# One of four softmax tiles in every other head has its low half made by GpSimd instead of VectorE

## The reference, cut to what matters

```python
scores = jnp.einsum('bhqd,bhkd->bhqk', q, k) / np.sqrt(Q_HEAD)
attn = jax.nn.softmax(scores, axis=-1)
o = jnp.einsum('bhqk,bhkv->bhqv', attn, v)
out = jnp.einsum('bhsv,Hv->bsH', o, Wo) + bo
```

## Time and profile before

| | |
|---|---|
| median of 3 runs | 1705.82 us (1705.19 to 1707.86) |
| the profiled execution's own time | 1698.23 us |
| its span in the trace | 1696.4 us |
| mean granted clock of TensorE | 0.989 of full speed |
| busy: PE, DVE, ACT, POOL | 95%, 90%, 81%, 56% |

### The profile page before, as it was taken

The page is one execution under the profiler, slowest core; times in us unless marked ns, Lnnn a source line. Parts: engine busy times, 40 slices in busy tenths (PEclk is TensorE's granted clock), DMA queues, the critical chain, the costliest instruction groups (busy, mean ns, idle before and its releaser), DMA issues. The chain is left out here.

```text
span 1696.4 us, 24098 instructions
## 1 busy us (share of the span) xinstructions
PE 1617.4 (95%) x7572; PEld 758.7 (45%) x7572; DVE 1522.8 (90%) x2080; ACT 1371.2 (81%) x1979; POOL 942.5 (56%) x1610
## 2 busy tenths in 40 slices
PE   7979899999999999999999999999999999999899
PEld 6734344444444444444444444444444444444344
DVE  5569898999998999999989999999989999999765
ACT  5668788888887889888979888988879888898422
POOL 3346555666655666666646655665545665564320
PEclk9989999999999999999999999999999999999999
DMA  6469999999999999999989999999999999999611
GB/s 218 155 115 211 203 199 205 206 201 187 201 195 166 201 202 200 200 198 196 202 160 203 196 199 198 199 200 198 196 165 196 204 198 199 194 194 201 145 50 50
DMA packets 1090457, 314.10 MB, mean 185 GB/s; under 512 B 1068352, under 2 KB 1078880, under 8 KB 1090336
## 3 DMA queue, kind: packets, MB, share of 16 engines
q1 hardware_dynamic: 1084288, 296.09, 94.8%
q0 software_dynamic: 6048, 16.52, 4.2%
HBM read 35.71 MB, written 8.39 MB: 26 GB/s over the span
## 5 line engine op out<-in xcount | busy, mean ns | idle before, releaser
L952 ACT ACTIVATE S<-S,shift,unscale 128x1024 f32<-128x1024 f32 x512 | 606.2, 1184 | 145.6 <-DVE shift L1007 144.3
L1000 DVE TENSOR_REDUCE mx<-S 128x1 f32<-128x1024 f32 x512 | 623.2, 1217 | 49.7 <-PE S L851 35.2
L992 DVE TENSOR_TENSOR halves<-S,halves 128x1024 f16<-128x1024 f32 x512 | 623.2, 1217 | 27.7 <-ACT halves L961 15.0
L961 ACT ACTIVATE halves<-S 128x1024 f16<-128x1024 f32 x512 | 526.1, 1027 | 26.0 <-DMA PT<-halves 14.2
L849 PE MATMUL S<-kvTH,qeH 128*128 128x512 f16 x1024 | 396.7, 387 | 19.7 <-DVE halves L992 17.9
L850 PE MATMUL S<-kvTL,qeH 128*128 128x512 f16 x1024 | 391.3, 382 | 0.0
L851 PE MATMUL S<-kvTH,qeL 128*128 128x512 f16 x1024 | 391.0, 382 | 0.0
L787 POOL CAST onormH<-onorm 128x512 fp32r<-128x512 f32 x127 | 77.6, 611 | 488.4 <-DVE onorm L1047 488.4
L862 PE MATMUL O<-PT,kvn 128*128 128x512 f16 x1024 | 241.9, 379 | 0.0
L849 PEld LDWEIGHTS S<-kvTH,qeH 128*128 128x128 f16 x1024 | 99.5, 97 | 255.9 <-DVE halves L992 145.3
L789 POOL TENSOR_TENSOR onormL<-onorm,onormH 64x512 fp32r<-64x512 f32 x127 | 163.6, 1288 | 10.2
(11 more groups left out here) (263 smaller groups left out, 1989.4 us busy)
## 6 DMA issues: line engine op xcount, KB each, us to landing
weff_whole<-weff_scratch POOLq DMA_DIRECT2D x126, 128.0 KB, 4.6
PT<-halves SPq DMA_TRANSPOSE x512, 4.9
raw<-in_raw SPq DMA_DIRECT2D x8, 772.0 KB, 5.9
weff_scratch<-w_split SPq DMA_DIRECT2D x8, 512.0 KB, 6.3
x<-in_x SPq DMA_DIRECT2D x4, 1024.0 KB, 8.3
x_all<-in_x SPq DMA_DIRECT2D x3, 1024.0 KB, 6.4
out<-y SPq DMA_DIRECT2D x3, 1024.0 KB, 4.3
wv<-in_wv SPq DMA_DIRECT2D x4, 512.0 KB, 5.1
```

The costliest lines, as they stand in the source:

```text
L952: nc.scalar.activation(S[:, t % SLOTS, :], S[:, t % SLOTS, :], ACT.Exp, bias=shift[:, col:col + 1], scale=keep["unscale"][:, 0:1], accum_o ...
L961: nc.scalar.activation(halves[u][:, 0, :], S[:, t % SLOTS, :], ACT.Copy).then_inc(high_out, 1)
L992: v.tensor_tensor(halves[u][:, 1, :], S[:, t % SLOTS, :], halves[u][:, 0, :], ALU.subtract).then_inc(low_out, 1)
L1000: v.reduce_max(mx[:, col:col + 1], S[:, t % SLOTS, :], AX.X, negate=True).then_inc(max_ready, 1)
```

## The change

In heads with even g ("pooled" heads, `pools(g)`) the exponential of tile 0 is written to `prob0`, a 128 x 1024 float32 view of `xn2` in SBUF, instead of its PSUM slot. `high(g,0)` reads it there. The low half of that tile is then made by GpSimd, right behind `onormL`, and raises a semaphore of its own, `low0_out`. VectorE leaves that one low out. SyncE's first turn of an even head waits for `low0_out`. TensorE's scores that reuse the slot of that tile wait for `probs_ready`, since nothing reads the slot after the exponential. The next pooled exponential waits for the last `low0_out`, and so does the use of `xn2` at the very end. Odd heads are as before. The function `lows(t)` counts the lows that VectorE still makes.

```diff
--- before.py
+++ after.py
@@ -617,6 +617,8 @@
 
         halves = [sb(f"halves{i}", [P, 2, SEQ], F16) for i in range(UN)]
         PT = [sb(f"PT{i}", [P, 2 * KEYT, BLK], F16) for i in range(2)]
+
+        prob0 = keep["xn2"][:, 0:2, :].rearrange("p t d -> p (t d)")
         wvs = sb("wv_scaled", [KVL, VH])
 
 
@@ -634,10 +636,10 @@
         turned = [sem(f"turned{i}") for i in range(UN)]
         weff_next = [sem(f"weff_next{i}") for i in range(2)]
         names = ("bv_in", "ones_set", "scores_ready", "max_ready", "shift_ready", "probs_ready",
-                 "high_out", "low_out", "recip_ready", "row_filled", "pv_done", "onorm_ready", "wv_done", "vsum_out",
+                 "high_out", "low_out", "low0_out", "recip_ready", "row_filled", "pv_done", "onorm_ready", "wv_done", "vsum_out",
                  "wv_split", "weff_high", "weff_split", "onorm_high", "onorm_low", "ffn_in", "row_ready", "bo_added", "projected0", "summed0",
                  "stats0", "std0_done", "rstd0_done", "sign_ready", "q_filled", "q_high", "q_copied", "q_low", "row_out")
-        (bv_in, ones_set, scores_ready, max_ready, shift_ready, probs_ready, high_out, low_out,
+        (bv_in, ones_set, scores_ready, max_ready, shift_ready, probs_ready, high_out, low_out, low0_out,
          recip_ready, row_filled, pv_done, onorm_ready, wv_done, vsum_out,
          wv_split, weff_high, weff_split, onorm_high, onorm_low, ffn_in, row_ready, bo_added, projected0, summed0,
          stats0, std0_done, rstd0_done, sign_ready, q_filled, q_high, q_copied, q_low, row_out) = (sem(n) for n in names)
@@ -658,6 +660,14 @@
 
         def exists(g):
             return 0 <= g < NG
+
+
+        def pools(g):
+            return g % 2 == 0
+
+        def lows(t):
+            g, u = t // UN, t % UN
+            return (2 * UN - 1) * (g // 2) + (u if pools(g) else UN + u)
 
         @block.sync
         def _(sp):
@@ -674,7 +684,10 @@
 
             def turn(g, u, par):
 
-                sp.wait_ge(low_out, UN * g + u + 1)
+                if u or not pools(g):
+                    sp.wait_ge(low_out, lows(UN * g + u))
+                else:
+                    sp.wait_ge(low0_out, g // 2 + 1)
                 sp.dma_start(PT[par][:, :, u * P:(u + 1) * P], halves[u][:].rearrange("p t s -> p (t s)"),
                              transpose=True).then_inc(turned[u], 16)
 
@@ -787,6 +800,9 @@
                     nc.gpsimd.tensor_copy(onormH[:], onorm[:]).then_inc(onorm_high, 1)
                     pool.wait_ge(onorm_high, g - 1)
                     nc.gpsimd.tensor_tensor(onormL[:], onorm[0:KVL, :], f32(onormH[0:KVL, :]), ALU.subtract).then_inc(onorm_low, 1)
+                if exists(g) and pools(g):
+                    pool.wait_ge(high_out, UN * g + 1)
+                    nc.gpsimd.tensor_tensor(halves[0][:, 1, :], prob0, halves[0][:, 0, :], ALU.subtract).then_inc(low0_out, 1)
                 if exists(g + 3):
                     split_weights(g + 3)
                 if exists(g + 5):
@@ -840,8 +856,10 @@
                     t = UN * g + u
                     if u == 0:
                         pe.wait_ge(q_low, g + 1)
-                    if t >= SLOTS:
-                        pe.wait_ge(low_out, t - SLOTS + 1)
+                    if t >= SLOTS and ((t - SLOTS) % UN or not pools((t - SLOTS) // UN)):
+                        pe.wait_ge(low_out, lows(t - SLOTS))
+                    elif t >= SLOTS:
+                        pe.wait_ge(probs_ready, t - SLOTS + 1)
                     q = slice(u * P, (u + 1) * P)
                     for c in range(2):
                         keys = slice((b // 2) * SEQ + c * BLK, (b // 2) * SEQ + (c + 1) * BLK)
@@ -898,7 +916,7 @@
                 if on:
                     scores(1)
                 if g == NG:
-                    pe.wait_ge(low_out, UN * NG - 1)
+                    pe.wait_ge(low_out, lows(UN * NG - 2))
                     project_tile(UN - 1)
                 if exists(g - 2):
                     values()
@@ -946,10 +964,15 @@
             copy_q(1)
 
             def body(g, b, h, par):
+                def probabilities(u):
+                    return prob0 if u == 0 and pools(g) else S[:, (UN * g + u) % SLOTS, :]
+
                 def exp(u):
                     t, col = UN * g + u, par * UN + u
                     act.wait_ge(shift_ready, t + 1)
-                    nc.scalar.activation(S[:, t % SLOTS, :], S[:, t % SLOTS, :], ACT.Exp, bias=shift[:, col:col + 1],
+                    if g and u == 0 and pools(g):
+                        act.wait_ge(low0_out, g // 2)
+                    nc.scalar.activation(probabilities(u), S[:, t % SLOTS, :], ACT.Exp, bias=shift[:, col:col + 1],
                                          scale=keep["unscale"][:, 0:1],
                                          accum_out=rs[:, col:col + 1]).then_inc(probs_ready, 1)
 
@@ -958,7 +981,7 @@
                     act.wait_ge(probs_ready, t + 1)
                     if g:
                         act.wait_ge(turned[u], 16 * g)
-                    nc.scalar.activation(halves[u][:, 0, :], S[:, t % SLOTS, :], ACT.Copy).then_inc(high_out, 1)
+                    nc.scalar.activation(halves[u][:, 0, :], probabilities(u), ACT.Copy).then_inc(high_out, 1)
 
                 def copy_row(out):
                     act.wait_ge(row_filled, g)
@@ -1052,7 +1075,7 @@
                         if u == 1 and one:
                             low(UN * g - 1)
                         shifted(u)
-                        if u == 1:
+                        if u == 1 and not pools(g):
                             low(UN * g)
                         if u == 1 and one:
                             reciprocals()
@@ -1082,6 +1105,7 @@
                     dve.wait_ge(std0_done, 1)
                     v.reciprocal(keep["rstd0"][:], keep["std0"][:]).then_inc(rstd0_done, 1)
                     dve.wait_ge(rstd0_done, 1)
+                    dve.wait_ge(low0_out, NG // 2)
                     for t in range(UN):
                         v.tensor_scalar(keep["xn2"][:, t, :], keep["x0"][:, t, :], keep["mv0"][:, t, 0:1],
                                         keep["rstd0"][:, t:t + 1], ALU.subtract, ALU.mult)
```

## The result

The changed kernel takes 1722.57 us (median of 4 runs, 1717.52 to 1729.49) against 1705.88 us for the kernel before. The ratio is 1.0102, with a 95% interval of 1.0071 to 1.0132: one per cent slower. Its profiled execution took 1718.9 us with a span of 1717.1, so it is 20.7 us above the profiled execution of before.

A forecast was written before the change was run, and what follows sets the result against it. The prediction took a ScalarE-VectorE loop to bound the kernel, with TensorE almost as tight. 60 x (0.31 gained - 0.20 for pauses) = 6.6 us, off the 1705.8 us median, gave 1699.3 us; range 1685 to 1717.

The forecast's parts named there:

- what bounds the kernel: One loop through ScalarE and VectorE, 11.25 us a head, including low(g,0); TensorE almost as tight, waiting 0.31 us for onormL.
- the gain: Removing VectorE's low of tile 0 saves 0.31 us in each of 60 even heads, 18.6 us in all.
- the new instruction: GpSimd's 128x1024 subtraction in even heads, taken as 2.2 us, with 2.1 to 2.6 kept as range.
- turn 0 of the even head: Issued 3.2 us late behind the new GpSimd row, landing 4.4 us later, 0.5 us before high(g+1,0) needs it.
- One small sum: New GpSimd row at 2.4 us, not 2.2: turn 0's margin 0.3 us and some 2 us less gain.
- the price of the pauses: Transfers pausing at instruction-code fetches delay turn 0 or 1 of even heads, costing 0.2 us a pair.
- The stretch: Time in a pair when a pause delays turn 0 or turn 1: about 4.4 + 3.3 = 7.7 us.
- The price of one: One 1.3 us transfer pause in that stretch costs 0.8 us at most, 0.7 on average.
- the fifth to a third: Expected sign: share of odd heads where ScalarE's high waits for PT<-halves, up to 1 us each.
- The odd head: Its turns find the queue shorter again; the 3 us backlog is worked off before the next even head.
- The first: Rival: transfer pauses miss the sensitive stretch, leaving the full 18.6 us gain, 1687.2 us; chance 0.17.
- The third rival: Slower: turn 0 late in every pair through longer GpSimd row and landing, 1717 to 1729 us; chance 0.23.

The follow-up runs named there:

- the run with two sets and the other order: Changed kernel with two sets of halves for even and odd heads, and even heads' turns issued 1, 0, 2, 3: 1689.84 us, ratio 0.9905.
- other order: Changed kernel, one set of halves, with SyncE issuing the turns of even heads in the order 1, 0, 2, 3: 1816.41 us, ratio 1.0643.
- late turn alone: Kernel before, VectorE making every low, plus an unused GpSimd subtraction every other head that turn 0 waits for: 1801.22 us, ratio 1.0563.
- low first: Changed kernel, one set of halves, with the GpSimd low ahead of the splitting of onorm, not behind it: 1695.62 us, ratio 0.9943.

## Why the prediction was wrong

I forecast 1699.3 us with a range up to 1717. The measured 1722.57 lies above it.

**Right: what bounds the kernel, and the gain.** Undisturbed pairs take 22.16 us, against 22.5 - 0.31 = 22.2 forecast. The wait of TensorE for `onormL` shrank as described. That the loop was really what held the kernel is shown by the run with two sets and the other order, in which nearly all pairs are of that length and the time is 1% lower.

**Right: the new instruction and turn 0 of the even head.** 2.14 us where 2.2 was taken. Turn 0 issued behind it, 4.4 us to land, 0.5 us of margin. The instruction alone and the exponential in SBUF alone change nothing that can be told, so neither is the cause. One small sum was off: by the forecast's own working, 0.2 us less margin costs 0.28 x 0.2 x 60 = 3 us, not 2.

**Wrong: the price of the pauses, 0.2 us a pair.** This is the term that failed: "The stretch in which one delays turn 0 or turn 1 is about 4.4 + 3.3 = 7.7 us, and it costs 1.3 - 0.5 = 0.8 us at most ... 0.2 us a pair". The mean pair of the changed kernel takes 22.85 us, 0.69 more than the undisturbed 22.16. So 0.31 - 0.20 = +0.11 us became 22.54 - 22.85 = -0.31 us a pair. Over 64 pairs that is 20 us, about the whole difference of 20.7 us between the profiled executions. Three things were too small in it, and a fourth was left out.
- The stretch. Of the 48 pairs, 30 had a 16 KB fetch in the 12.4 us of the table. In the forecast's own 7.7 us, from 4.9 to 12.6 us behind `onorm`, there were 20, a share of 0.42 where 0.8 x 7.7 / 22.2 = 0.28 was forecast. They average 23.16 us. A pause counts also when it comes before turn 0 is issued: the 8 pairs whose only 16 KB fetch came between 2 us before `onorm` and 4.9 us behind it average 22.98.
- The other queue of code. The earlier trace rows show the 61 packets of q8 alone. A second queue, q14, fetched as many packets of half the size. Pairs with only such packets take 22.78 against 22.34 us.
- The price of one. Against the 22.20 us of a pair with no fetch, a large fetch in the forecast's own stretch cost 1.0 us, where 0.7 was taken. Of 54 odd heads 21 waited for turn 0 and 26 for turn 1, more than the fifth to a third that I gave.
- The odd head, which the sum put at nothing. I wrote that its turns "find the queue shorter again". Its turn 0 had a median margin of 0.1 us (3.1 before), and of the 54 even heads from 20 on, 17 waited for the odd head's turn 0, 15.1 us in all, against 20.2 us of the odd heads for turn 0 of the even ones. How much of that is hidden in ScalarE's idle time is not known.

**The rivals.** The first (pauses do not matter) is contradicted by the lengths of pairs of the changed kernel; before the change it was true, since 39 pairs with and without fetch took 22.49 us, and the other 9 average 22.74 only by one pair of 24.71. The Trainium skill's "Runtime: NRT & Kernel Launch" ("Instruction fetch mechanics") calls the cost of crossing a block of code mostly hidden: the trace agrees for the kernel before and not for the changed one, whose pairs are 0.65 us longer on average (22.85 against 22.20) than those with no fetch. The third rival named the right side and the right wait, `high(g+1,0)` for turn 0, and its time of 1717 to 1729 holds the measured 1722.57. Its mechanism was another: it made turn 0 late in every pair by a longer instruction and landing, and 21 of 54 odd heads waited.

**What remains.** That lateness of turn 0 is the loss is shown by four runs: 2 us of it cost 1.9 (other order), making turn 0 late with nothing saved costs 5.6% (late turn alone), a turn 2.7 us earlier removes the loss (low first), and a second buffer for tile 0 alone removes it. The last of these freed the even and the odd heads at once, so the runs do not tell how the loss divides between the even head's turn 0 and the odd head's. That the pauses come from the fetches, and that they set off the lateness, is seen in the lengths of pairs and in single heads, but no run changed the number of large fetches. Nearly the whole 0.69 us (0.65) is missing in pairs with no fetch, which is a strong association and not an experiment. The late turn alone warns that a backlog without any fetch can be as dear. The mean pair falls from 22.85 to 22.59 us with tile 0 doubled, and to 22.49 with tiles 0 and 1.

## What to carry to other kernels

When work is moved off a loop that sets the pace, ask what the slower engine's result releases, and how far the next user of that buffer is away. A margin of 0.5 us that holds in a clean stretch isn't a margin if the thing waited for is stopped for 1.3 us at irregular times; sum all such pauses and compare them with the slack, not with the stretch that looks sensitive. Follow the backlog into the next unit of work too, here the odd head, until it is worked off. And place the instruction by its deadline: the same instruction a few lines earlier in GpSimd's body was worth 1.6%.

## What the runs showed of the hardware

- Behind a 16 KB fetch of instruction code the transposing transfers stood still for 1.35 us, behind an 8 KB one for 0.45 us (medians of 41 and 37 cases in the kernel before; counted are stretches of 0.2 us and more under 40 GB/s with a turn under way, at most 1 us behind the fetch). Beside the 128 KB load of query weights, with no fetch, they stood still for 0.45 us (median of 103).
- The exponential of 128x1024 from PSUM took 1.23 us into SBUF and 1.18 into PSUM, the copy to float16 1.06 us from SBUF and 1.02 from PSUM (medians of the changed kernel). VectorE's subtraction took 1.22 us from either.
- GpSimd's 128x1024 subtraction, float32 minus float16 into float16, took 2.13 to 2.15 us in all 64 cases, beside whatever VectorE did.
